# Delta attention: Gram products in tiles of 64 rows and columns from four masked copies of the keys

## The reference, cut to what matters

```python
def delta_attn(x, Wq, Wk, Wv, Wb, Wo, onorm_w):
    q = l2norm(silu(x @ Wq)); k = l2norm(silu(x @ Wk)); v = silu(x @ Wv)   # per head
    beta = sigmoid(x @ Wb) * 2.0
    def step(S, inps):
        qi, ki, vi, bi = inps
        pred = einsum('bhkv,bhk->bhv', S, ki)
        S = S + bi * ki[..., :, None] * (vi - pred)[..., None, :]
        return S, einsum('bhkv,bhk->bhv', S, qi)
    ...
x = input_embeds.transpose(1, 0, 2)
for l in range(2):
    h = rmsnorm(x, norm1_w[l]); x = x + delta_attn(h, ...)
    h = rmsnorm(x, norm2_w[l]); g, y = split(h @ Wg[l]); x = x + silu(g) * y @ Wd[l]
```

## Time and profile before

| | |
|---|---|
| Time, median of 3 runs | 2700.44 us (2696.92 to 2703.26) |
| The profiled execution: its time | 2704.79 us |
| The profiled execution: its span | 2703.0 us |
| Instructions in the span | 44,428 |
| Busy: PE, PEld, DVE, ACT, POOL | 74%, 52%, 44%, 30%, 14% of the span |

### The profile page before, as it was taken

One profiled execution on the slowest core, in us unless ns is written; L12 is line 12 of the kernel. 1 busy time (PEld: TensorE's weight loads), 2 busy tenths in 40 slices (PEclk: granted clock), 3 DMA queues, 4 the chain that ended last, 5 costly groups with the idle time before them and its releaser, 6 DMA issues. The chain is left out here.

```text
span 2703.0 us, 44428 instructions
## 1 busy us (share of the span) xinstructions
PE 2009.9 (74%) x17299; PEld 1411.0 (52%) x17316; DVE 1186.8 (44%) x2480; ACT 815.0 (30%) x1468; POOL 389.2 (14%) x597
## 2 busy tenths in 40 slices
PE   5769479799999876999710678999566767537777
PEld 3536245466676555776500466767455555325554
DVE  3347444433555565111279552111566485333232
ACT  1126124222222254344100453343312402223332
POOL 1233232000000131000100420000143061110000
PEclk7659689799999877999855688999768877559998
DMA  1012110000000020000000210000000000000000
GB/s 51 0 48 60 31 41 26 25 24 0 30 19 25 20 84 23 11 21 16 5 0 0 74 41 9 16 23 8 28 2 0 2 1 1 12 0 0 0 0 16
DMA packets 35843, 53.47 MB, mean 20 GB/s; under 512 B 4225, under 2 KB 29569, under 8 KB 35329
## 3 DMA queue, kind: packets, MB, share of 16 engines
q1 hardware_dynamic: 33378, 49.13, 6.1%
q10 hardware_dynamic: 2304, 2.10, 0.3%
HBM read 25.00 MB, written 1.05 MB: 10 GB/s over the span
## 5 line engine op out<-in xcount | busy, mean ns | idle before, releaser
L1747 ACT ACTIVATE l2f_a<-l2f_bank,l2f_expert 128x512 f32<-128x512 f32 x144 | 99.0, 687 | 148.8 <-PE l2f_bank L1709 148.4
L1720 PEld LDWEIGHTS l2f_bank<-l2f_expert,l2f_a 128*128 128x128 f32 x1152 | 132.9, 192 | 12.9 <-issue 12.9
L1766 DVE SCALAR_TENSOR_TENSOR X<-l2f_bank,l2f_W,X 128x128 f32<-128x128 f32 x144 | 40.7, 344 | 221.5 <-PE l2f_bank L1720 221.4
L1709 PE MATMUL l2f_bank<-l2f_xT,l2f_expert 128*128 128x512 f32 x288 | 130.7, 602 | 5.3 <-PE l2f_bank L1720 4.2
L1720 PE MATMUL l2f_bank<-l2f_expert,l2f_a 128*128 128x128 f32 x1152 | 133.0, 275 | 0.0
L1747 ACT ACTIVATE l1f_a<-l1f_bank,l1f_expert 128x512 f32<-128x512 f32 x128 | 87.9, 687 | 131.1 <-PE l1f_bank L1709 131.1
L1720 PEld LDWEIGHTS l1f_bank<-l1f_expert,l1f_a 128*128 128x128 f32 x1024 | 118.1, 192 | 11.5 <-issue 11.5
L1991 POOL TENSOR_TENSOR l3a_KE<-l3a_W,l3a_GQ 128x128 f32<-128x128 f32 (+15 forms) x32 | 102.6, 3230 | 146.0 <-DVE l3a_W L2369 139.1
L1766 DVE SCALAR_TENSOR_TENSOR X<-l1f_bank,l1f_W,X 128x128 f32<-128x128 f32 x128 | 36.0, 344 | 197.4 <-PE l1f_bank L1720 197.4
L2092 PE MATMUL l3a_bank<-l3a_KE,ident 128*128 128x128 f32 x544 | 87.6, 330 | 45.6 <-POOL l3a_KE L1991 45.2
L1709 PE MATMUL l1f_bank<-l1f_xT,l1f_expert 128*128 128x512 f32 x256 | 116.5, 604 | 4.7 <-PE l1f_bank L1720 3.6
(11 more groups left out here) (602 smaller groups left out, 4345.4 us busy)
## 6 DMA issues: line engine op xcount, KB each, us to landing
l2f_expert<-in_experts_l2f SPq DMA_DIRECT2D x9, 514.0 KB
l1a_layer<-in_layers_l1a SPq DMA_DIRECT2D x12, 385.0 KB
l1f_expert<-in_experts_l1f SPq DMA_DIRECT2D x8, 514.0 KB, 3.5
l0x_k_stack<-l0x_k_parts SPq DMA_DIRECT2D x48, 64.0 KB
l0g_k_stack<-l0g_k_parts SPq DMA_DIRECT2D x48, 64.0 KB
l0f_expert<-in_experts_l0f SPq DMA_DIRECT2D x4, 768.0 KB, 4.6
l1x_k_stack<-l1x_k_parts SPq DMA_DIRECT2D x48, 64.0 KB
l2x_k_stack<-l2x_k_parts SPq DMA_DIRECT2D x48, 64.0 KB
```

The source lines that it names most:

```text
L1709: pe.matmul(self.banks[c][:, :], self.buf[b][:, c * P:(c + 1) * P], x, start=True, stop=True)\
L1720: ins = pe.matmul(out[:, i * D:(i + 1) * D], self.a[:, par, c, i * T:(i + 1) * T], w2[:, c, :], start=(c == 0), stop=(c == FC - 1))
L1747: act.activation(self.a[:, par, c, :], self.banks[c][:, :], ACT.Gelu, bias=self.buf[b][:, 2 * FF + c:2 * FF + c + 1]).then_inc(q["gated"], 1)
L1766: ins = dve.scalar_tensor_tensor(out=x, in0=self.banks[4 + h % 2][:, i * D:(i + 1) * D], scalar=self.W[:, h * GI + i, bass.ds(e, 1)], in1= ...
```

## The change

Each matmul of `products` takes 64 rows (four heads) and a stationary operand of 64 columns (four masked copies of 16 keys); the moving operand stays 32 columns wide. A step needs two matmuls in place of four, a layer 256 in place of 512. KE becomes twice as large, KQ and GT keep their size. `take_k` makes four masked copies of each group in place of two, with a step of 64 elements between neighbours in KE where there were 32. The tile sqk has no room of its own any more and lies in the last quarter of GT. The layout of the products in PSUM and everything after it stay.

```diff
-PACKS["l3a"] = Pack(("final", P, D), ("parity", P, 2))
+PACKS["l3a"] = Pack(("final", P, D), ("parity", P, 4))
...
-PAIR = 2
-TILE = 32
+PAIR = 4
+TILE = 64
+WIDE = 32
...
-    sqk = sb("sqk", [P, GI, 2 * D])
     KE = sb("KE", [P, T * TILE])
-    KQ = sb("KQ", [P, T * TILE])
-    GT2 = sb("GT", [P, T * TILE])
+    KQ = sb("KQ", [P, T * WIDE])
+    GT2 = sb("GT", [P, T * WIDE])
...
+    sqk = GT2[:, 3072:4096].rearrange("p (i d) -> p i d", i=GI)
...
-                        at = (c * NB + t) * TILE
+                        at, to = (c * NB + t) * TILE, (c * NB + t) * WIDE
                         for r in range(0, P, TILE):
-                            ins = pe.matmul(b[c % 4][r:r + TILE, t * TILE:(t + 1) * TILE], KE[r:r + TILE, at:at + TILE],
-                                            KQ[r:r + TILE, at:at + TILE], start=True, stop=True)
+                            ins = pe.matmul(b[c % 4][r:r + TILE, t * WIDE:(t + 1) * WIDE], KE[r:r + TILE, at:at + TILE],
+                                            KQ[r:r + TILE, to:to + WIDE], start=True, stop=True)
```

## The result

| | Before | After |
|---|---|---|
| Time, median of 14 runs each | 2696.94 us (2688.82 to 2703.26) | 2713.15 us (2708.21 to 2720.08) |
| Ratio | 1 | 1.0061, 95% interval 1.0051 to 1.0072 |
| Profiled execution: time, span | 2704.79, 2703.0 us | 2716.52, 2714.7 us |

The account below looks back on a forecast made before the run. Instruction fetch was taken to bound `products`. Per layer, 3.62 us of copies plus 1.0 or 1.3 us of longer loads made 9.5 us in all: 2714.3 us profiled, 2710 us on the median; range 2698 to 2718 us.

Parts of the forecast that it names:

- The fetch of instructions is the bound before, and is gone after: `products`: blocks of 128 records every 3.52 us before; after, four blocks, 14.0 us of fetch, hidden behind the array.
- A pair costs 106.7 ns: `products`: 64-column loads set the pace, both tiles overlapping; 256 pairs take 27.5 us, +1.0 and +1.3 us.
- Masked copies at 0.905 us: VectorE before `products`: two more copies per group, 1.81 us; first two groups hidden, last two paid, +3.62 us a layer.
- The clock stays at 0.50: TensorE in `products`: small tiles don't bring the clock up, so the granted clock remains 0.50.
- the gapless stretch at 0.57: 32-row matmuls without a gap, 4.64 us, granted 0.57; cited as evidence that small tiles don't raise the clock.
- Rival 1: `products`, L2062: pair costs half (53.3 ns), fetch again the bound, stage 14.0 us; 2683 us in all; 11%.
- in front of products: TensorE's waits for the added masked copies of the third and fourth groups: +3.62 us in a layer.
- Rival 3: `products`: the two tiles take turns, 512 x 106.7 ns = 54.6 us a layer; +64 us, 2764 us; 3%.
- rival 4: VectorE's masked copies: the wider step is dearer, 1.8 us a copy; +30 us with the array's part, 2731 us; 4%.

## Why the prediction was right, step by step

The direction, the likeliest time (2710 against 2713.15 us) and the range held. The size was too small: 9.5 us or 1.0035 was forecast, 16.2 us or 1.0061 measured, and the interval begins at 1.0051. That the likeliest time came within 3 us is partly luck: it was counted from 2700.44 us, the median of three runs, and over 14 runs the kernel before stands at 2696.94. These 3.5 us too many cover half of the 6.7 us that the sum lacked.

- **The fetch of instructions is the bound before, and is gone after.** Right. Shown by each product twice and by the old tiles at a clock of 1.0. The pace was read as one block every 3.52 us; the traces have 3.47, 3.75 and 4.02, so what the old stage is compared with moves by 1.7 us.
- **A pair costs 106.7 ns, `products` 27.5 us.** Right, 27.52 us; that the load alone sets it was shown by the wider moving operand.
- **Masked copies at 0.905 us, the first two groups hidden, the last two paid.** Right: 0.90 us, waits of 4.75 and 4.70 us where 4.8 and 4.7 were said, +3.6 us in a layer by themselves.
- **The clock stays at 0.50.** Right for the kernel as it stands, but the reason was wrong. I gave the small tiles as the cause, from the gapless stretch at 0.57. That row was misread: the granted clock is 0.99 over its first 0.63 us (29.67 to 30.30) and 0.50 behind them, so the stretch shows a clock that fell. The same 32 matmuls ran at a clock of 1.00 from start to end elsewhere in the kernel before:

```profile
105.29 2.82 PE L1064 MATMUL l0a_bank<-l0a_qT,l0a_kT 32*128 32x128 f32 x32 [1.62 <-POOL l0a_kT L1031]
```

So small tiles at a high clock could be seen before the change. The new tiles with 32 moving columns did not lift the clock in any of the six stages that began at 0.50 (27.52 us each), and held it in three of the four that began at 1.0. What the stage lacked was a high clock at its start, behind two idle waits. Rival 1 at 11% was one edit away.
- **What was missing in the sum.** The term "in front of products" was sized at 7.2 us and measured 9.9 (4.7 and 5.2). In the first layer the clock fell within the longer wait, and the last transposes of keys and queries take 0.9 us more (1957.03 to 1958.96 in place of 1953.91 to 1954.97). In the second, the projection of the third group ran at the low clock (4.54 us where 2.85 stood), 1.7 us, in both traces of the changed kernel. That is not from the longer wait, which comes behind it. The run with old tiles and filled waits, the one with filled waits on the changed kernel and the one with both tiles have 4.54 us there as well, and those with four copies and with a wider operand don't; why is open.
- **Behind the stage.** VectorE's solve of the second layer (from its first to its last instruction, L2365 to L2369 in the kernel before) takes 67.6 us in the two traces with the old products and 65.0 in both of the changed kernel, so 2.6 us are given back. It is not the new tiles that do it: the solve takes 64.9 and 65.1 us there in two runs with the old tiles (shared copies, wide moving operand), and 67.6 in the changed kernel's run with copies on ScalarE. What makes it 65 or 67.6 us was not tried. From the kernel before to the changed one the pieces are: in front +9.9, products +2.3, from their ends to the last matmul of the solve +0.8 and -2.5, the rest of the layers 0; 10.6 us for this pair.
- **What stays open.** The sublayer is 10.4 us longer. The runs say 16.2 and 14.3. The 4 to 6 us between lie outside of the sublayer or in the choice of the profiled executions. The sublayers behind it, which no edit touches, take 399.2 and 392.4 us in the two old traces, 399.2 and 395.8 in the two new, at a granted clock of 0.81, 0.83, 0.81 and 0.82: one trace differs from the next there by more than what is missing. The sublayer is no finer: in the run with four copies it is 10.7 us longer than before, and the runs say 8.2. The places of the tiles are excluded. No run tells more.

Rival 3 (tiles in turn) and rival 4 (a dearer step) are excluded by the 27.52 and the 0.90 us.

## What to carry to other kernels

Where TensorE shows gaps put down to "issue" in long straight code of small matmuls, and instruction packets at the same pace, ask what the array would need without them before making the matmuls larger: here it needed as much (27.5 against 26.3 us), because a larger stationary operand takes longer to load. Two limits at the same height have to be lowered together. Read the clock of the stage and the wait in front of it: the same products took 15.1 us when the wait was filled with matmuls on the full array (one stage of four fell back to 25.3), and with that the change that had cost 0.6% gained 0.6%.

## What the runs showed of the hardware that was not expected

- Tiles of 64 rows and columns with a moving operand of 32 kept a clock of 0.50 for 27.5 us without a gap, and kept a clock of 1.0 for 15.1 us, if it stood there at the start (three of the four stages behind filled waits; in the fourth it fell some 3 us in).
- The same tiles with a moving operand of 64 columns raised the clock from 0.50 to 1.0 within 4 us, and so made the stage 11 us shorter with more work in it. Tiles of 32 with 64 moving columns raised it as well.
- Straight code of small matmuls got its instructions in packets of 16 KB, one for 128 records and their loads, 3.47, 3.75 or 4.02 us apart, at a clock of 0.50 and of 1.0 alike.
- Tiles of 32 rows and 128 columns held a clock of 1.00 for 2.82 us in one place of the kernel before and lost it after 0.6 us in another.
- ScalarE took 1.25 us for a masked copy of 128x512 from SBUF to a stepped place where VectorE took 0.90 from PSUM.
